# Attention over 40,000 edges: scaling the gathered rows on ScalarE, whole one-hots on VectorE, and the next group's scores ahead of the sums

## What is computed

```python
h = node_feats @ W
s_l = h @ a_l
s_r = h @ a_r
logits = s_l[src] + s_r[dst]
e = jnp.exp(-jax.nn.leaky_relu(logits, negative_slope=ALPHA))
row_sum = jax.ops.segment_sum(e, src, num_segments=N)
h_prime = jax.ops.segment_sum(e[:, None] * h[dst], src, num_segments=N)
return jax.nn.elu(h_prime / row_sum[:, None])
```

## Time and profile before

| | us |
|---|---|
| Median of 3 runs (2719.55 to 2726.37) | 2723.11 |
| The profiled execution, its own time | 2718.02 |
| Span of the profiled execution | 2716.3 |

### The profile page before, as it was taken

One profiled execution on the slowest core, in us unless ns is written; L12 is line 12 of the kernel. 1 busy time (PEld: TensorE's weight loads), 2 busy tenths in 40 slices (PEclk: granted clock), 3 DMA queues, 4 the chain that ended last, 5 costly groups with the idle time before them and its releaser, 6 DMA issues. The chain is left out here.

```text
span 2716.3 us, 46328 instructions
## 1 busy us (share of the span) xinstructions
PE 2088.1 (77%) x13095; PEld 1804.4 (66%) x13096; DVE 1647.1 (61%) x4774; ACT 1007.2 (37%) x1931; POOL 1394.8 (51%) x1131
## 2 busy tenths in 40 slices
PE   2599999999999999955629999990466666662778
PEld 2588888888888888855628888880444444441776
DVE  5477786666666666648464444445655555557774
ACT  1254445545445554432205555550222222221321
POOL 1387887877777877760001111105377777771000
PEclk9799999999999999977759999995777767765888
DMA  6466656666666666642116777762233333342001
GB/s 165 134 131 131 133 120 130 134 132 135 135 128 125 133 130 133 129 86 70 39 41 229 244 243 242 239 220 81 76 92 93 90 89 91 90 84 28 22 10 38
DMA packets 185998, 325.71 MB, mean 120 GB/s; under 512 B 27528, under 2 KB 109037, under 8 KB 185192
## 3 DMA queue, kind: packets, MB, share of 16 engines
q0 software_dynamic: 82080, 141.73, 25.8%
q1 hardware_dynamic: 102962, 181.83, 21.8%
q10 hardware_dynamic: 900, 1.50, 0.2%
HBM read 260.65 MB, written 64.30 MB: 120 GB/s over the span
## 5 line engine op out<-in xcount | busy, mean ns | idle before, releaser
L632 POOL DMA_INDIRECT edge_sums<-edge_agg,edge_slot x316 | 551.3, 1745 | 172.5 <-issue 78.8
L1750 POOL DMA_INDIRECT att_got<-head_table,att_idx x352 | 401.8, 1141 | 125.1 <-issue 107.0
L623 POOL DMA_INDIRECT edge_nf<-node_table,edge_node_idx x316 | 327.3, 1036 | 152.0 <-issue 89.0
L751 ACT ACTIVATE edge_whole<-edge_h_ps,edge_b 128x512 f32<-128x512 f32 x316 | 215.8, 683 | 482.2 <-PE edge_h_ps L468 478.4
L466 PE MATMUL edge_e_ps<-edge_w_high,edge_hid_low 128*128 128x256 f32 x1264 | 357.3, 283 | 0.1
L467 PE MATMUL edge_e_ps<-edge_w_low,edge_hid_high 128*128 128x256 f32 x1264 | 356.9, 282 | 0.0
L468 PE MATMUL edge_e_ps<-edge_w_high,edge_hid_high 128*128 128x256 f32 x1264 | 356.2, 282 | 0.0
L1780 PE MATMUL att_s_ps<-att_w,att_hot 128*125 128x258 f32 x704 | 277.0, 562 | 3.2 <-issue 1.8
L466 PE MATMUL edge_h_ps<-edge_eat_high,edge_w_low 128*128 128x512 f32 x632 | 248.9, 394 | 23.6 <-DVE edge_eat_low L811 23.6
L1361 POOL DMA_INDIRECT moe_rows<-node_table,moe_idx x54 | 51.9, 961 | 396.8 <-DVE moe_idx L1473 396.4
L825 DVE TENSOR_TENSOR edge_pre<-edge_e_ps,edge_nf 128x1024 f32<-128x1024 f32 x79 | 96.8, 1225 | 256.2 <-DMA edge_nf<-node_table,edge_node_idx 208.9
(11 more groups left out here) (344 smaller groups left out, 4424.4 us busy)
## 6 DMA issues: line engine op xcount, KB each, us to landing
moe_w<-in_L_ffn_w_dram SPq DMA_DIRECT2D x162, 512.0 KB, 4.7
edge_ea<-in_edge_attr_dram SPq DMA_DIRECT2D x77, 448.0 KB, 5.1
edge_dst_row<-dst_rows SPq DMA_DIRECT2D x79, 256.0 KB, 4.5
routed<-moe_out SPq DMA_DIRECT2D x54, 128.0 KB, 6.3
att_got<-head_table,att_idx POOLq DMA_INDIRECT x352, 2.8
edge_nf<-node_table,edge_node_idx POOLq DMA_INDIRECT x316
edge_sums<-edge_agg,edge_slot POOLq DMA_INDIRECT x316, 4.8
edge_ea<-in_edge_attr_dram SPq DMA_DIRECT2D x77, 64.0 KB, 5.3
```

Source lines behind the costliest of these rows:

```text
L623: pool.indirect_dma_start(nf[u][:, j, :], None, m.node_table[:, :], bass.IndirectOffsetOnAxis(ap=node_idx[u][:, j:j + 1], axis=0)).then_in ...
L632: pool.indirect_dma_start(m.sums[k][:, :], bass.IndirectOffsetOnAxis(ap=slot[u][:, j:j + 1], axis=0), agg[u][:, j, :], None, compute_op=AL ...
L751: act.activation(whole[c][:], h_ps[:, c % 2, 0:N], ACT.Relu, bias=b1[:, c:c + 1]).then_inc(hid_whole, 1)
L1750: pool.indirect_dma_start(got[v][:, j, :], None, m.head_table[:, :], bass.IndirectOffsetOnAxis(ap=idx[v][:, j:j + 1], axis=0)).then_inc(la ...
```

## The change

ScalarE takes over the scaling: eight activations with Copy (four blocks, two heads), each of 128 x 128 numbers with one scale for each partition, read from `w`, where the exponential is now written directly. The tile `e` and the copy L1841 are gone. ScalarE no longer widens the one-hots: VectorE makes them a second time, whole, in float32 (`one_hots_whole`). ScalarE's order for each g becomes: the exponential of g, the copy of `hot_t` of g + 1 (`take_turned`), the eight scalings of g. VectorE's order becomes: the bf16 one-hots of g + 1, the indices of g + 4, the logits of g + 1, the sums of g - 1, the whole one-hots of g + 1. A gather now also waits until the scaling of its buffer four groups back is done. TensorE's code is the same.

```diff
@@ gpsimd
+                    if begun(g, RB):
+                        pool.wait_ge(scaled, g - (RB - 1))
@@ scalar
-                def one_group(g, u, begun=True):
+                def take_turned(g, u):
                     act.wait_ge(turned, g + 1)
                     nc.scalar.activation(hot_t[u][:], t_ps[0:LANES, :, :], ACT.Copy).then_inc(turned_in, 1)
-                    if begun:
+
+                def exponentials(g, u):
+                    act.wait_ge(lrelu_ready, g + 1)
+                    if begun(g, 2):
                         act.wait_ge(scattered, g - 1)
-                    nc.scalar.activation(hot[u][:], hot16[u][:], ACT.Copy).then_inc(hot_ready, 1)
-                    act.wait_ge(lrelu_ready, g + 1)
-                    nc.scalar.activation(e[u][:], lrelu[u][:], ACT.Exp, scale=-1.0).then_inc(e_ready, 1)
+                    nc.scalar.activation(w[u][:, :, DIM:ROW], lrelu[u][:], ACT.Exp, scale=-1.0).then_inc(e_ready, 1)
+
+                def scale_rows(g, u, v):
+
+                    act.wait_ge(e_ready, g + 1)
+                    for j in range(G):
+                        for h in range(HEADS):
+                            part = slice(h * HEAD_C, (h + 1) * HEAD_C)
+                            last = nc.scalar.activation(w[u][:, j, part], got[v][:, j, part], ACT.Copy, scale=w[u][:, j, DIM + h:DIM + h + 1])
+                    last.then_inc(scaled, 1)
+
+                def one_group(g, v):
+                    u = v % 2
+                    exponentials(g, u)
+                    if left(g, 1, groups):
+                        take_turned(g + 1, 1 - u)
+                    scale_rows(g, u, v)
@@ vector
+                def one_hots_whole(g, u):
+                    if begun(g, 2):
+                        dve.wait_ge(scattered, g - 1)
+                    for j in range(G):
+                        last = nc.vector.tensor_scalar(hot[u][:, j, :], m.count16[:, 0:LANES],
+                                                       r.lane[:, bass.DynSlice(g * G + j, 1)], None, ALU.is_equal)
+                    last.then_inc(hot_ready, 1)
@@ vector, logits
+                    if begun(g, 2):
+                        dve.wait_ge(e_ready, g - 1)
@@ vector, one_group
                     if left(g, 1, groups):
-                        if not start:
-                            dve.wait_ge(hot_ready, g)
                         one_hots(g + 1, 1 - u)
-                    scale_rows(g, u, v)
                     if left(g, RB, groups):
                         stage_idx(g + RB, v)
+                    if left(g, 1, groups):
+                        logits(g + 1, 1 - u, (v + 1) % RB)
                     if not start:
                         accumulate(g - 1, 1 - u, first)
                     if left(g, 1, groups):
-                        logits(g + 1, 1 - u, (v + 1) % RB)
+                        one_hots_whole(g + 1, 1 - u)
```

More of the change, by code:

```diff
@@ L1735, in attend_edges @@
         lrelu = sb("lrelu", [P, G, HEADS])
-        e = sb("e", [P, G, HEADS])
         w = sb("w", [P, G, ROW])
@@ L1751, in gather @@
                                                 bass.IndirectOffsetOnAxis(ap=idx[v][:, j:j + 1], axis=0)).then_inc(landed[v], 16)
-                with pool.Fori(0, turns) as i:
+                for v in range(RB):
+                    gather(v, v)
+                with pool.Fori(1, turns) as i:
                     for v in range(RB):
@@ L1798, in _ @@
             def _(act):
-                def one_group(g, u, begun=True):
+                def take_turned(g, u):
                     act.wait_ge(turned, g + 1)
                     nc.scalar.activation(hot_t[u][:], t_ps[0:LANES, :, :], ACT.Copy).then_inc(turned_in, 1)
-                    if begun:
+                def exponentials(g, u):
+                    act.wait_ge(lrelu_ready, g + 1)
+                    if begun(g, 2):
                         act.wait_ge(scattered, g - 1)
-                    nc.scalar.activation(hot[u][:], hot16[u][:], ACT.Copy).then_inc(hot_ready, 1)
-                    act.wait_ge(lrelu_ready, g + 1)
-                    nc.scalar.activation(e[u][:], lrelu[u][:], ACT.Exp, scale=-1.0).then_inc(e_ready, 1)
+                    nc.scalar.activation(w[u][:, :, DIM:ROW], lrelu[u][:], ACT.Exp, scale=-1.0).then_inc(e_ready, 1)
[12 more added lines that the diff above has]
+                    scale_rows(g, u, v)
+                take_turned(0, 0)
                 for v in range(RB):
-                    one_group(v, v % 2, v >= 2)
-                with act.Fori(1, turns) as i:
+                    one_group(v, v)
+                with act.Fori(1, turns - 1) as i:
                     for v in range(RB):
-                        one_group(RB * i + v, v % 2)
+                        one_group(RB * i + v, v)
+                for v in range(RB):
+                    one_group(groups - RB + v, v)
             @block.vector
@@ L1819, in one_hots @@
                 def one_hots(g, u):
+                    if begun(g, 2):
+                        dve.wait_ge(turned, g - 1)
                     for j in range(G):
@@ L1870, in _ @@
                 one_hots(0, 0)
+                one_hots_whole(0, 0)
                 logits(0, 0, 0)
```

## The result

The changed kernel takes 2803.07 us, the median of 4 runs (2800.80 to 2806.12), against 2722.35 us before; the ratio is 1.0296, with a 95% interval of 1.0278 to 1.0314. It is slower by 81 us. The profiled execution took 2806.12 us with a span of 2804.3.

A forecast was written before the change was run, and what follows sets the result against it. GpSimd bounds the kernel before; afterwards a ScalarE-TensorE chain of 7.00 us a group does. The stage takes 9 + 87 x 7.00 + 5 = 623 us against 527, so 2723 + 96 = 2819 us, range 2780 to 2855.

The forecast's parts named there:

- GpSimd sets the pace before, and the multiply stretches the gathers: Stage before: 352 gathers need 441 us on GpSimd; VectorE's two-tensor multiply stretches them by 66 us more.
- Eight scalings take 2.44 us: ScalarE, each group: 7 x 0.293 + 0.39 = 2.44 us, priced from f16 activations in L373; bounds 2.1 and 3.1.
- The closed chain of ScalarE and TensorE: Each group: transposes, ScalarE's copy, eight scalings, scatter, next transposes in turn; 7.39 us at lower clock, 5.42 at higher.
- The clock's part: TensorE's scatter at the lower clock 80% of the time, against 63% before, giving 7.00 us a group.
- the prediction's own formula: TensorE's lower-clock share from the scatter's mean weight load: (278 - 183)/(333 - 183) = 63% before the change.
- the sum: One group's chain at the lower clock: 0.72 + 0.50 + 2.44 + 0.14 + 3.59 = 7.39 us.
- the mean clock would fall below 0.71: Sign in the stage: TensorE's mean granted clock, 0.71 before, would be lower in the changed kernel.
- VectorE's own chain: From source scores through logits, sums and both one-hots: 3.3 us beside TensorE's 3.8 or 5.6 us, so practically no cost.
- rival A's second half: If the chain did not bind, GpSimd's 441 us would: kernel about 2657; chance of both halves together 0.09.
- The cost of moving the whole one-hots to VectorE: VectorE's float32 one-hots, 0.75 us a group, cost nothing as long as TensorE and ScalarE need over 4 us.

The follow-up runs named there:

- the early reads: Changed kernel with only VectorE's two reads of tile numbers moved ahead of its wait for the source scores: 2800.77 us, ratio 1.0317.
- the run with both edits: Changed kernel with ScalarE's copy behind the eight scalings and VectorE's tile-number reads ahead of its wait for source scores: 2661.41 us, ratio 0.9796.

## Why the prediction was right, and where it was not

The time (2819 forecast, 2803 measured) and the direction were right, and for the reason given.

- **GpSimd sets the pace before, and the multiply stretches the gathers.** Shown by the runs without the multiply and with eight one-tensor multiplies. Of the 66 us of stretching, 64 and 59 came out of the stage (61 and 53 us by the ratios of the whole). The inference of the Trainium skill ("SBUF — State Buffer", "Who interferes with whom"), that such an instruction leaves descriptor generation alone, does not hold for these indirect gathers: 2.1 against 0.95 us when a gather begins together with the multiply. The prediction leaves out that the timing decides: with the multiply back beside the new order, only 8 gathers took over 1.2 us.
- **Eight scalings take 2.44 us.** Measured 2.43. The f16 row of another stage was a good price for the float32 form.
- **The closed chain of ScalarE and TensorE.** Shown by the order on ScalarE alone (-36 us, then hidden by the next chain; -140 us with the early reads) and by the count of scalings: four wide ones in place of eight -60, four more +142.
- **The clock's part was mis-sized in both directions.** By the prediction's own formula the scatter's weight loads (316 ns on the mean, between 183 and 333) were 89% at the lower clock, where I had 80%. But the transposes ran at the higher clock (0.39 us, as in the earlier trace rows), where the sum had them at 0.69 in most groups, and the last part of the scatter too (3.34 against 3.59). The clock changes within each group. Stretches of two groups, each from the transposes on and then inside the scatter (as in the earlier trace rows, with the clock third from the end):

```profile
2203.52:2206.00 2.48, 0.72 (x9) 0.48 (x7) 0.51 (x3) 2.05 (x7) 1.83 (x2) 1.00 0.37 107
2207.00:2210.00 3.00, 3.00 (x7) 2.42 (x8) 2.56 (x11) 0.00 (x0) 1.95 (x2) 0.50 0.15 45
2210.32:2213.00 2.68, 0.71 (x9) 0.47 (x7) 0.52 (x3) 2.25 (x8) 1.80 (x2) 1.00 0.35 99
2213.80:2216.80 3.00, 2.89 (x7) 2.31 (x8) 2.57 (x11) 0.00 (x0) 1.96 (x2) 0.50 0.16 44
```

It rises near the end of the scatter and has fallen by the time the next begins. The prediction's picture was another, four groups in five slow throughout and the fifth fast. In its place 77 of the 88 groups have six or seven of their eight scatter loads at the lower clock. So the group took 6.8 to 6.9 us instead of 7.00, and nearly the same one each time. The stage came to 608 us instead of 623, which is the 16 us between forecast and result. That it came so near is in part luck: with 89% in the prediction's formula a group would take 7.17 us and the kernel 2834, and the transposes and the end of the scatter, cheaper than in the sum, took that back and more. I had also said that the mean clock would fall below 0.71; it is 0.74. A stage's mean tells too little here: the clock was at its higher level in stretches in which TensorE worked 0.72 of 2.48 us, and those do not shorten the scatter.
- **VectorE's own chain: the step that failed.** I put it at 3.3 us, with 0.2 us for reading registers, and at nothing as long as TensorE took over 4 us. From the source scores' parts (2205.05) to the end of the bf16 one-hots (2209.92) it is 4.87 us: the reads cost 1.48 us in front of the sums and the float32 one-hots 0.94. The 0.2 us came from an order in which a long instruction ran over the reads. The change takes that cover away twice: it removes the instruction (without the multiply, in the order of before, the gap is there in 59 groups), and it puts the logits between (with the multiply back, the gap is still 1.46 us). Here it was harmless, since 6.42 is less than 6.80. But rival A's second half, that GpSimd's 5.01 us would bind if ScalarE's chain did not, was wrong for that reason: with ScalarE's chain gone the kernel is still at 2767. Its 2657 is what came once both chains were gone (2661).
- **The cost of moving the whole one-hots to VectorE**, put at nothing, was right in the order of before: that run took 0.9969 of the time.

## What to carry to other kernels

When work moves between engines, write down the closed chain that each new order makes (what an engine waits for, what is queued behind it, who waits for that): an engine that is 44% busy, as ScalarE with 268 of 608 us, can be half of the bound. Two such chains hide each other, so an edit that gains nothing alone may be worth 4% beside another; take out the longer one first and look again. Before moving work off an engine, try another form of the same instruction where it is: eight one-tensor multiplies in place of one two-tensor multiply gave 2% by themselves, as much as the mended change (2666 and 2661).

## What the runs showed of the hardware that was not expected

- Eight multiplies of 128 x 128 float32 by a scalar for each partition take 1.67 us on VectorE, against 1.22 for the one with two tensors, and leave gathers at 0.953 us on the median, 1.157 at most, where the one made them up to 2.165.
- One and the same 1.2 us multiply held 66 gathers beyond 1.2 us in the kernel before and 8 in the run with the multiply back. In the trace of before, the held ones are those that began while it ran or up to 0.10 us ahead of it.
- Two register reads on VectorE with nothing long issued before them held its next instruction back by 1.47 us, in 86 groups of 88 (126.5 us in the changed kernel). Issued ahead of a wait for TensorE they left no such gap (the run with both edits), and a 1.2 us multiply issued just before them, with no wait between, covered all but 0.2 us of them.
- In the changed kernel TensorE's clock is at 0.74 on the mean over the stage, and the scatter's loads, at 316 ns on the mean, still lie at 89% of the way from the higher clock's 183 ns to the lower one's 333. In the run with four more scalings TensorE waited over 3 us before each scatter, its loads took 326 ns on the mean (95% by the same measure), and each group lost 0.4 us beyond what was added.
